# GpSimd rounds rows of 704 numbers in two halves of 352: six instructions in place of three

## The reference

```
x = x + attention(layernorm(x))      # q, k with rotary positions, causal softmax, output projection
x = x + ffn(layernorm(x))

def fp4_quant_dequant(x):            # blocks of 16 along the last dimension
    scale = max(max(|block|) / 6.0, 1e-12)
    idx = searchsorted(_MID, |block / scale|)
    return _GRID[idx] * sign(block) * scale        # grid 0, 0.5, 1, 1.5, 2, 3, 4, 6

def fp4_linear(x, w):
    return einsum('bsk,nk->bsn', fp4_quant_dequant(x), fp4_quant_dequant(w))

gate, y = fp4_linear(x, w_gate), fp4_linear(x, w_up)     # 256 -> 704
h = silu(gate) * y
return fp4_linear(h, w_down)                             # 704 -> 256
```

## Time and profile before

| | |
|---|---|
| median of 3 runs | 1302.66 us (1300.41 to 1303.75) |
| the profiled execution, its own time | 1298.29 us |
| its span in the profile | 1296.5 us |
| mean granted clock of TensorE | 0.983 of full |
| PE busy | 1219.2 us (94%) |
| DVE busy | 1097.2 us (85%) |
| ACT busy | 763.1 us (59%) |
| POOL busy | 470.5 us (36%) |
| chain that ended last | PE 70%, DVE 16%, ACT 6%, issue 3%, POOL 2%, DMA 2% |

### The profile page before, as it was taken

The page is one execution under the profiler, slowest core; times in us unless marked ns, Lnnn a source line. Parts: engine busy times, 40 slices in busy tenths (PEclk is TensorE's granted clock), DMA queues, the critical chain, the costliest instruction groups (busy, mean ns, idle before and its releaser), DMA issues.

```text
span 1296.5 us, 40306 instructions
## 1 busy us (share of the span) xinstructions
PE 1219.2 (94%) x16886; PEld 689.7 (53%) x16886; DVE 1097.2 (85%) x2946; ACT 763.1 (59%) x1658; POOL 470.5 (36%) x501
## 2 busy tenths in 40 slices
PE   7679999899999999999999999999999999999867
PEld 6445555455555555555466555545545555554345
DVE  5799998889898999979479989899998999985066
ACT  4346776456564676656655655646565675656721
POOL 2944665553221112131445562332221112023145
PEclk9879999899999999999999999999999999999989
DMA  4734222311001101101023222111011100000000
GB/s 105 177 96 118 72 78 62 92 30 43 16 21 38 31 2 43 27 10 36 14 64 91 67 67 60 35 34 39 11 30 35 35 2 19 2 6 14 13 13 17
DMA packets 63937, 57.28 MB, mean 44 GB/s; under 512 B 17534, under 2 KB 57344, under 8 KB 63744
## 3 DMA queue, kind: packets, MB, share of 16 engines
q1 hardware_dynamic: 60728, 53.62, 15.9%
q10 hardware_dynamic: 3028, 1.09, 0.3%
HBM read 37.51 MB, written 16.78 MB: 42 GB/s over the span
## 4 chain that ended last, share of the span: by engine, by line
PE 70%; DVE 16%; ACT 6%; issue 3%; POOL 2%; DMA 2%; ACTq 1%; SPq 0%; DVEq 0%; POOLq 0%
PE bank L920 14%; PE bank L932 14%; PE bank L875 13%; PE bank L896 12%; PE bank L1044 7%; DVE bank L1279 6%; ACT prob L1177 5%; DVE piece_max L1282 4%; PE bank L991 4%; PE bank L1035 2%; PE bank L999 2%; PE bank L927 1%; DVE piece_max L1279 1%; PE bank L1006 1%; PE bank L901 1%
## 5 line engine op out<-in xcount | busy, mean ns | idle before, releaser
L1177 ACT ACTIVATE prob<-bank 128x512 f32<-128x512 f32 (+3 forms) x1280 | 594.5, 542 | 280.2 <-PE bank L896 172.6
L1282 DVE TENSOR_REDUCE piece_max<-bank 128x1 f32<-128x512 f32 x768 | 488.1, 676 | 7.1 <-PE bank L875 6.1
L896 PE MATMUL bank<-q_mem,k_mem 99*32 99x512 bf16 (+13 forms) x5120 | 383.9, 341 | 10.6 <-DMA q_mem<-max_rows 8.1
L875 PE MATMUL bank<-k_mem,q_mem 96*32 96x512 bf16 (+14 forms) x5120 | 381.5, 344 | 9.3 <-DVE piece_max L1279 5.5
L920 PE MATMUL bank<-prob,V 128*32 128x512 f32 (+3 forms) x2560 | 293.8, 531 | 15.6 <-ACT prob L1177 11.9
L1496 POOL TENSOR_TENSOR c_mem<-c_mem 128x256 f32<-128x256 f32 (+2 forms) x74 | 85.0, 1149 | 420.3 <-DVE c_mem L1370 420.3
L875 PEld LDWEIGHTS bank<-k_mem,q_mem 96*32 96x32 bf16 x5120 | 135.4, 96 | 182.8 <-issue 104.1
L896 PEld LDWEIGHTS bank<-q_mem,k_mem 99*32 99x32 bf16 x5120 | 145.3, 96 | 152.9 <-issue 65.4
L1279 DVE CUSTOM_DVE_ANT_0 bank<-bank,past_keys 128x32 f32<-128x32 f32 (+15 forms) x512 | 207.9, 468 | 2.8 <-PE bank L875 2.5
L920 PEld LDWEIGHTS bank<-prob,V 128*32 128x32 f32 x2560 | 70.6, 110 | 67.3 <-ACT prob L1177 30.0
L901 PE MATMUL bank<-mask_kq,ident_h 128*32 128x128 bf16 (+3 forms) x2048 | 100.7, 200 | 0.0
(11 more groups left out here) (173 smaller groups left out, 1394.5 us busy)
## 6 DMA issues: line engine op xcount, KB each, us to landing
parts_dram<-a_mem SPq DMA_DIRECT2D x13, 512.0 KB, 3.5
q_mem<-parts_dram SPq DMA_DIRECT2D x32, 192.0 KB, 2.9
k_mem<-parts_dram SPq DMA_DIRECT2D x32, 192.0 KB, 3.5
q_mem<-parts_dram SPq DMA_DIRECT2D x32, 128.0 KB, 3.0
k_mem<-parts_dram SPq DMA_DIRECT2D x32, 128.0 KB, 3.5
c_mem<-in_L_attn_x SPq DMA_DIRECT2D x30, 128.0 KB, 2.1
out<-c_mem SPq DMA_DIRECT2D x30, 128.0 KB, 1.7
a_mem<-in_L_attn_x SPq DMA_DIRECT2D x13, 256.0 KB, 2.8
```

Of the source, the lines that this page charges most:

```text
L875: m = pe.matmul(b[COLUMNS * h:COLUMNS * (h + 1), of], q_rows(u)[0:TERM_ROWS, h, block * COLUMNS:(block + 1) * COLUMNS], k_rows(k0 // CHUNK ...
L896: mm = pe.matmul(b[k0:k0 + COLUMNS, since:CHUNK], k_rows(j // TPC, g)[:, h, first:first + COLUMNS], q_rows(u)[:, h, since:CHUNK], start=Tr ...
L1177: act.activation(prob[:, n % NP, off:CHUNK], bank_of("st", n)[:, off:CHUNK], ACT.Exp, scale=SCALE).then_inc(drained("st", n)[0], 1)
L1282: r = dve.tensor_reduce(most, scores, AX.X, ALU.max)
```

## The change

Rows of 704 are split in two halves of 352 numbers (22 blocks of 16), and each of the three POOL steps is issued once for each half. The order is first step of both halves, second step of both, third step of both; each waits for the step before it of its own half. PE waits for all six. The plan is told of the same six steps, each at 150 ns + 2.1 (1.7 for the last) ns for each of 352 numbers, where it had three at 150 + 2.1 (1.7) times 704.

```diff
+    def grid_halves(width):
+        return 2 if width == FF else 1
...
-        for n in range(3):
-            yield from plan.step("pool", ("grid", n) + key, 150 + (2.1 if n < 2 else 1.7) * width, last)
-            last = [("grid", n) + key]
+        halves = grid_halves(width)
+        for n, half in itertools.product(range(3), range(halves)):
+            yield from plan.step("pool", ("grid", n, half) + key, 150 + (2.1 if n < 2 else 1.7) * width / halves,
+                                 [("grid", n - 1, half) + key] if n else last)
...
-        yield from plan.through(("hT0", t), 440, "act", 493, [("grid", 2, "h", t)])
-        yield from plan.through(("hT1", t), 220, "act", 265, [("grid", 2, "h", t)])
+        yield from plan.through(("hT0", t), 440, "act", 493, [("grid", 2, 1, "h", t)])
+        yield from plan.through(("hT1", t), 220, "act", 265, [("grid", 2, 1, "h", t)])
...
-        TILE_VECTOR, TILE_POOL, TILE_SCALAR = 15, 9, 2
+        TILE_VECTOR, TILE_POOL, TILE_SCALAR = 15, 12, 2
...
-                at.wait_ge(ffn_pool[s], c_pool[t] + 9)
+                at.wait_ge(ffn_pool[s], c_pool[t] + TILE_POOL)
...
+                halves = grid_halves(width)
+                each = width // halves
+                nb = each // FP4_BLOCK
+                for n, half in itertools.product(range(3), range(halves)):
+                    at_, of = slice(half * each, (half + 1) * each), slice(half * nb, (half + 1) * nb)
+                    a, b, to = v["qa"][0:rows, at_], v["qb"][0:rows, at_], dst[:, at_]
+                    yield when[("grid", n, half) + key]
+                    if n == 0:
+                        at.wait_ge(*rounded)
+                        pool.tensor_tensor(a, a, b, ALU.add).then_inc(done, 1)
+                    elif n == 1:
+                        at.wait_ge(done, first + half + 1)
+                        pool.tensor_tensor(a, a, b, ALU.subtract).then_inc(done, 1)
+                    else:
+                        at.wait_ge(done, first + halves + half + 1)
+                        pool.tensor_tensor(
+                            to.rearrange("p (n f) -> p n f", f=FP4_BLOCK), a.rearrange("p (n f) -> p n f", f=FP4_BLOCK),
+                            v["scale"][0:rows, of].unsqueeze(2).broadcast_to([rows, nb, FP4_BLOCK]),
+                            ALU.mult).then_inc(done, 1)
```

More of the change, by code:

```diff
@@ L1 @@
+import itertools
 from contextlib import ExitStack
@@ L441, in rehearse_weights @@
                 yield from rehearse_rounding(("w", n), width, ready)
-                ready = [("grid", 2, "w", n)]
+                ready = [("grid", 2, grid_halves(width) - 1, "w", n)]
             for part in range(weight_parts[n]):
@@ L487, in rehearse_feed_forward @@
         yield from rehearse_rounding(("x", t), D, [("f xn", t)])
-        yield from plan.through(("xT", t), 222, "act", 280, [("grid", 2, "x", t)], [("wo", t)])
+        yield from plan.through(("xT", t), 222, "act", 280, [("grid", 2, 0, "x", t)], [("wo", t)])
         for half in range(2):
@@ L643, in preln_layer @@
         vector_steps, pool_steps, scalar_steps = [0] * NC, [0] * NC, [0] * NC
-        for n, (_, _, _, quantised, _, _) in enumerate(ffn_weights):
+        for n, (_, _, width, quantised, _, _) in enumerate(ffn_weights):
             s = w_set[n]
@@ L649, in preln_layer @@
                 vector_steps[s] += 6
-                pool_steps[s] += 3
+                pool_steps[s] += 3 * grid_halves(width)
         for s in range(NC):
@@ L948, in ffn_weight @@
                 if quantised:
-                    at.wait_ge(ffn_pool[w_set[n]], w_pool[n] + 3)
+                    at.wait_ge(ffn_pool[w_set[n]], w_pool[n] + 3 * grid_halves(width))
                 stage = C[w_set[n]][w_slot[n]]
@@ L1490, in deviation, with quantise @@
                                    ALU.pow).then_inc(done, 1)
-            def quantise(key, rows, width, v, dst, done, first):
-                nb = width // FP4_BLOCK
-                a, b = v["qa"][0:rows, 0:width], v["qb"][0:rows, 0:width]
-                pool.tensor_tensor(a, a, b, ALU.add).then_inc(done, 1)
-                yield when[("grid", 1) + key]
-                at.wait_ge(done, first + 1)
-                pool.tensor_tensor(a, a, b, ALU.subtract).then_inc(done, 1)
-                yield when[("grid", 2) + key]
-                at.wait_ge(done, first + 2)
-                pool.tensor_tensor(
-                    dst.rearrange("p (n f) -> p n f", f=FP4_BLOCK), a.rearrange("p (n f) -> p n f", f=FP4_BLOCK),
-                    v["scale"][0:rows, 0:nb].unsqueeze(2).broadcast_to([rows, nb, FP4_BLOCK]),
-                    ALU.mult).then_inc(done, 1)
+            def quantise(key, rows, width, v, dst, done, first, rounded):
+                halves = grid_halves(width)
[17 more added lines that the diff above has]
+                            ALU.mult).then_inc(done, 1)
             def ffn_weight(n):
@@ L1509, in ffn_weight @@
                 s = w_set[n]
-                yield when["grid", 0, "w", n]
-                at.wait_ge(ffn_vector[s], w_vector[n] + 6)
-                yield from quantise(("w", n), m, width, C[s], C[s][w_slot[n]][0:m, 0:width], ffn_pool[s], w_pool[n])
+                yield from quantise(("w", n), m, width, C[s], C[s][w_slot[n]][0:m, 0:width], ffn_pool[s], w_pool[n],
+                                    (ffn_vector[s], w_vector[n] + 6))
             def copy_tables(z):
@@ L1550, in feed_forward @@
                                      when["f inverse", t])
-                yield when["grid", 0, "x", t]
-                at.wait_ge(ffn_vector[s], c_vector[t] + 9)
-                yield from quantise(("x", t), P, D, v, v["xn"], done, first + 3)
-                yield when["grid", 0, "h", t]
-                at.wait_ge(ffn_vector[s], c_vector[t] + 15)
-                yield from quantise(("h", t), P, FF, v, v["h"], done, first + 6)
+                yield from quantise(("x", t), P, D, v, v["xn"], done, first + 3, (ffn_vector[s], c_vector[t] + 9))
+                yield from quantise(("h", t), P, FF, v, v["h"], done, first + 6, (ffn_vector[s], c_vector[t] + 15))
             in_time(constants(), *(ffn_weight(n) for n in range(len(ffn_weights)) if ffn_weights[n][3]),
```

## The result

| | before | after |
|---|---|---|
| median of 15 runs each | 1305.38 us | 1315.21 us |
| lowest, highest | 1298.39, 1311.10 | 1307.90, 1322.65 |
| ratio, 95% interval | | 1.0071 [1.0049, 1.0094] |
| profiled execution: own time, span | 1298.3, 1296.5 | 1319.03, 1317.2 |
| mean granted clock in it | 0.983 | 0.970 |

The change costs some 9 us. The forecast of 1299.4 us and its range up to 1308 both missed. One caution for all that follows: the profiled execution of before lies near the low end of its runs and that of after lies above its median, so the two traces differ by 20.7 us where the medians differ by 9.8. The traces say where the time went, and the timed runs say how much.

A forecast was written before the change was run, and what follows sets the result against it. PE was taken as the bound, with only 77 us of idle to gain or add to; -4.0 - 8.8 + 8.8 + 0.7 = -3.3 us gave 1295.0, with a 4.4 us offset to the median 1299.4 us, range 1291 to 1308.

The forecast's parts named there:

- What the split may give back on DVE: Last tile's rounding: half of 1.91 us of waits inside DVE instructions saved, 0.95 us; in the middle such waits are hidden.
- The rival on the slower side: Middle loses feed-forward filler: over 200 us 7.3 us of idle added, +4.0 us in all, 1306.7 us; chance 0.20.
- The condition named at the end of the prediction: Forecast would be wrong if, among other things, the middle's idle, 14.9 us, moved by over 4 us either way.
- POOL's work: Each rounding on POOL: six 352-wide instructions take 5.37 us where three took 4.77; +0.60 us, used as 0.65.
- (a): End of attention, before the last `pv`: 11 unfilled steps become 3 by the order; 4.0 us gained.
- (b): Before the last `pv`: tile 27's `xT`, products, `hT` and `down` leave that part; 8.8 us.
- (c): Behind the last `pv`: tile 27's work comes back; the end grows by 8.8 us, from 59.9 to 68.7.
- The walk: PE's new order stepped through behind the last `pv`, all at the full clock, with its waits; end 68.7 us long.
- PE's clock drops at the end: Behind the last `pv`: waits bring PE's low clock level twice, 3.4 us lost, about 1302.8 us; chance 0.10.
- the sum: Whole kernel: -4.0 - 8.8 + 8.8 + 0.7 = -3.3 us.
- (d): Early rounding of w_down's two row blocks: one delay of 0.65 us on PE's path, +0.7; bounds 0 and 1.3.
- DVE's steps at the end: Last tile's rounding: DVE's division (1.95 us) and next step (1.37 us) lose half their waits, with smaller maxima.

The follow-up runs named there:

- e5: After, with a wait on the POOL instruction before added to eight POOL instructions of the run by 750 us only; 1309.32 us, 0.9998 of before.
- e11: After, with such waits at both places only, six POOL instructions by 193 us and eight by 750 us; 1304.05 us, 0.9979 of before.
- e3: After, with every POOL instruction waiting for the POOL instruction before it to end; 1308.06 us, 1.0010 of before.
- e1: Before's order, with each 704-wide POOL step issued as two halves, one right behind the other; 1309.71 us, 1.0006 of before.
- e9: The kernel before once more, nothing changed; 1305.67 us, 0.9994 of before.
- e4: Before, with every POOL instruction waiting for the POOL instruction before it to end; 1307.82 us, 1.0000 of before.
- e7: The kernel after once more, unchanged, profiled a second time; 1318.17 us, 1.0061 of before.
- e6: After, with a wait on the POOL instruction before added to six POOL instructions by 192 us only; 1310.61 us, 1.0020 of before.
- e2: After's order on every engine, but each POOL step whole (704 wide) instead of halves; 1311.86 us, 1.0038 of before.
- e10: Kernel without the layer: one DVE cast 0.2 to 1.2 us into five kinds of POOL run; no wait longer than one POOL instruction.
- e12: Kernel without the layer: one DVE cast 0.7 to 10 us into four kinds of POOL run; no wait longer than one POOL instruction.
- e13: Kernel without the layer: POOL's and DVE's own work by 750 us, ScalarE and TensorE busy; no wait longer than one POOL instruction.
- e8: Kernel without the layer: 24 DVE casts in a row beside whole or half POOL steps; no wait longer than one POOL instruction.

## Why the prediction was wrong

**The step that failed is "What the split may give back on DVE".** It took the waits inside DVE's instructions for a matter of the one POOL instruction in progress, halved them with its length, and said of the middle that "such waits are hidden: PE idles 1.6% there". At two places of 1317 us DVE waited until the fifth and the ninth POOL instruction had ended, and the waits were not hidden: PE idled 2.55 us by 194 us and 6.78 by 750, where it is packed to 98%, with a granted clock of 0.91 from 740 to 800 us. Shown: breaking the run by 750 us alone brings the time back to before's (e5, 0.9998), breaking both gives 0.9979 (e11), and breaking all runs does no better (e3, 1.0010). Not shown: why these two and not the many others.

That step had rows for its belief. The earlier trace rows hold waits of 1.06 and 0.85 us beside POOL steps of 1.4 to 1.7 us, all within one instruction. They could not show what happens when POOL's queue never pauses, because in the tail before the change it pauses often. But the same trace had the addition by 123 us, 1.33 us through more than one POOL instruction, which the step left out. The rival on the slower side had the right place, the middle, and the wrong mechanism: it expected idle time spread over 200 us for want of filler. The idle time from 300 to 740 us is unchanged to 0.3 us and from 800 to 1211 to 0.8. The condition named at the end of the prediction, idle time of the middle that moves by over 4 us, is what came: 14.9 us are 22.7.

The other steps, in the two profiled executions:

- *POOL's work.* 352 wide: 950, 942 and 800 ns by the groups of after, so six take 5.38 us; 5.37 were worked out. POOL is busy 486.7 us in all, under the 490 to 495 named. e1 shows the split to be worth +0.06% within 0.18.
- *(a), 4.0 us gained.* From 1211 us to the last `pv` PE idled 5.54 us; in after it idles 2.1 in the 34 us to 1245. Gained 3.4.
- *(b), 8.8 us leave.* The last `pv` ended at 1244.88, not at 1222 to 1227: -8.8 of work, -3.4 of idle there, +12.0 of idle ahead, and 8.6 us more of matmuls for the same work, together +8.4; the timeline says +8.3. The 8.6 are the remainder of this pair of traces and no price of the change: up to the last `pv` PE was busy 1176.0 us in before, but 1178.1, 1185.1 and 1183.2 in e9, e1 and e4, which keep its order, and with the new order 1175.8 in after, 1171.3 in e3 and 1171.2 in e11. The last `pv` of these two ended at 1234.2 and 1232.4, still behind 1227.
- *(c), +8.8 us behind it.* The end grew by 12.4, to 72.3 us. PE's busy time there grew by 12.4 (43.17 to 55.55 us) and its idle time not at all (16.73 and 16.65). The walk was right in most of its waits: x of 28 at 1.78 us where 2.0 was predicted, h of 30 and 31 at 0.97 and 1.65 where it had 1.4 and 1.5. It was wrong in two: h of 27 cost 0.63 us where it had 2.1, and x of 29, which was to be ready before PE wants it, 1.07. The 3.6 us beyond 8.8 are matmuls at a low clock, such as the eight transposes of 1.94 us at 1247.44. That is the rival "PE's clock drops at the end", which was priced at 3.4 us and stood apart from the sum. In e3 against e4 the end grew by the 8.8 of the walk (62.9 to 71.7 us), and in e11 against e9 by 12.5 (61.2 to 73.7), so the clock's part is not steady between executions.
- *(d), +0.7.* The wait it was about, PE's for w_down's rounding, went the other way: 2.0 us before, 1.3 in after. In e1, which keeps before's order, it is 2.3, so the split alone added 0.3 to it.
- *DVE's steps at the end.* The longest L1364 and L1372 of the last three tiles take 1.09 and 0.93 us, where they took 1.95 and 1.37. There the halving did come.

With the two runs broken, e11 stands at -0.21% [-0.44, +0.03] where -0.25% was forecast for the change. That agrees with the sum, but the interval is too wide to call the sum confirmed, and e3, which also has the new order and no long waits, stands at +0.1%. The parts don't agree: against e9 the last `pv` of e11 ends 6.3 us earlier, where 12.1 were forecast, and its end is 12.5 us longer, where 8.8 were. So the agreement of the total may be luck.

## What to carry to other kernels

When a change makes one engine's queue run without pauses, look at who shares something with it: search the trace for single instructions many times longer than their like, and sum not their mean but their longest. The waits that were already satisfied broke no run here; a wait on the engine's own last instruction, at the few places where the long ones stand, cost nothing here and gave back the whole loss. And don't read a price of the clock from one pair of traces: the window from 740 to 800 us fell to a clock of 0.91 behind the long wait, but over all timed runs the clock of after (0.974) and before (0.975) hardly differs.

## What the runs showed of the hardware

- A DVE instruction of 0.17 us can last 7.97 us beside nine POOL instructions without a pause, and the place repeats: 7.97, 7.81 and 7.78 us by 750 us in three traces (after, e7, e6), 4.59, 4.57, 4.60 and 4.15 us by 193 us in four (after, e7, e1, e2). It isn't chance of one execution.
- Waits beyond the instruction in progress need no change of order: an addition of 0.10 us takes 1.33 or 1.34 us by 123 us in eight traces, before's included, and 0.17 and 0.18 us in the two in which each POOL instruction waits for the one before.
- Long waits are rare all the same. In the 204 requests of e10, e12 and e13, 184 of them beside runs without a pause of up to 15 us, DVE never waited for more than one POOL instruction.
- Where it gets in at a boundary no cost to POOL can be seen: the six whole steps of e8 start every 1.62 us with a DVE cast at each boundary, and each takes 1.66 or 1.67 us.
